# Windowed attention, tile by tile: probabilities are divided by their sums, V becomes the stationary operand, and GpSimd adds the two products of the rotation

## The reference, cut to what matters

```
h = shift_token(x); q, k, v = split(h @ wqkv)        # 8 heads of 64
q, k = l2norm(q) * qs, l2norm(k) * ks
q = q*cos*scale + rotate_half(q)*sin*scale           # k with 1/scale
sim = 8 * q @ k.T, banded; attn = softmax(sim)
x = x + (attn @ v) @ wo
h = layernorm(shift_token(x)) * lg + lb; a, g = split(h @ w1 + b1)
x = x + (a * gelu(g)) @ w2 + b2
```

## Time and profile before

| | |
|---|---|
| median of 3 runs | 429.11 us (429.06 to 431.6) |
| the profiled execution's own time | 431.58 us |
| its span | 429.8 us |
| granted TensorE clock, mean | 0.956 |
| busy over the span: PE, DVE, ACT, POOL | 86%, 81%, 67%, 5% |

### The profile page before, as it was taken

The page is one execution under the profiler, slowest core; times in us unless marked ns, Lnnn a source line. Parts: engine busy times, 40 slices in busy tenths (PEclk is TensorE's granted clock), DMA queues, the critical chain, the costliest instruction groups (busy, mean ns, idle before and its releaser), DMA issues.

```text
span 429.8 us, 10211 instructions
## 1 busy us (share of the span) xinstructions
PE 371.4 (86%) x4104; PEld 272.0 (63%) x4104; DVE 349.4 (81%) x721; ACT 289.1 (67%) x602; POOL 22.8 (5%) x30
## 2 busy tenths in 40 slices
PE   2799999998556789997858999999999999997866
PEld 1488788886511435564435766876767687776845
DVE  5989978986888899886979889888797988884642
ACT  1789998884355457778354666867868777766641
POOL 2000020000020040000000000000000002020110
PEclk9999999999955999999999899999999999998997
DMA  8700010000000000000000000000000000000000
GB/s 325 302 4 4 3 41 3 3 4 3 1 0 1 2 0 2 2 2 0 2 1 2 0 2 0 2 2 0 2 2 1 2 0 2 2 0 2 25 2 24
DMA packets 1774, 8.30 MB, mean 19 GB/s; under 512 B 192, under 2 KB 448, under 8 KB 1472
## 3 DMA queue, kind: packets, MB, share of 16 engines
q1 hardware_dynamic: 1728, 7.65, 4.5%
HBM read 7.12 MB, written 0.52 MB: 18 GB/s over the span
## 4 chain that ended last, share of the span: by engine, by line
PE 48%; DVE 32%; ACT 14%; issue 5%; DMA 1%; DVEq 0%; ACTq 0%
PE ps L252 13%; PE ps L657 5%; ACT blk L1350 3%; PE ps L505 3%; DVE blk L1180 3%; PE ps L630 3%; DVE blk L1171 3%; DVE blk L1162 3%; PE ps L611 2%; PE ps L569 2%; DVE lneg L1187 2%; DVE ss L1172 2%; PE ps L621 2%; PE ps L583 2%; PE ps L492 2%
## 5 line engine op out<-in xcount | busy, mean ns | idle before, releaser
L569 PE MATMUL ps<-w_f,full 128*128 128x512 f32 x96 | 44.7, 599 | 1.4 <-issue 0.9
L1468 ACT ACTIVATE PT<-ps,lneg 128x128 f32<-128x128 f32 x128 | 34.6, 381 | 13.9 <-DVE lneg L1187 13.9
L630 PEld LDWEIGHTS ps<-blk,PT 128*128 128x128 f32 x256 | 30.3, 192 | 0.6
L630 PE MATMUL ps<-blk,PT 128*128 128x65 f32 x256 | 30.4, 272 | 0.0
L252 PEld LDWEIGHTS ps<-blk,st 128*128 128x128 bf16 x768 | 26.8, 98 | 3.8
L1162 DVE TENSOR_TENSOR blk<-ps,tabs 128x1024 f32<-128x1024 f32 x16 | 19.5, 1221 | 11.5 <-ACT blk L1435 11.2
L252 PE MATMUL ps<-blk,rel 128*128 128x64 bf16 x768 | 27.6, 193 | 0.0
L252 PE MATMUL ps<-blk,st 128*128 128x64 bf16 x768 | 27.6, 193 | 0.0
L569 PEld LDWEIGHTS ps<-w_f,full 128*128 128x128 f32 x96 | 16.9, 190 | 16.9 <-issue 16.7
L1022 DVE TENSOR_REDUCE mneg<-ps 128x4 bf16<-128x512 bf16 x32 | 21.9, 686 | 6.6 <-PE ps L357 6.4
L583 PEld LDWEIGHTS ps<-const,blk 128*128 128x128 f32 x128 | 14.8, 146 | 17.3 <-DVE blk L1180 14.6
(11 more groups left out here) (235 smaller groups left out, 913.9 us busy)
## 6 DMA issues: line engine op xcount, KB each, us to landing
w_f<-f_dram SPq DMA_DIRECT2D x2, 1689.0 KB, 13.3
w_x<-l_dram SPq DMA_DIRECT2D x1, 774.0 KB, 6.0
w_f<-ffn_dram SPq DMA_DIRECT2D x1, 561.0 KB, 8.0
X<-x_dram SPq DMA_DIRECT2D x1, 512.0 KB, 3.6
ctxT<-ctxT_dram SPq DMA_DIRECT2D x1, 512.0 KB, 4.5
OT<-maskT_dram SPq DMA_DIRECT2D x1, 512.0 KB, 7.1
rest<-l_dram SPq DMA_DIRECT2D x1, 385.0 KB, 4.2
const<-const_dram SPq DMA_DIRECT2D x1, 324.0 KB, 6.3
```

The costliest lines, as they stand in the source:

```text
L569: m = mm(ps[:, c, :], hT[:, n, :], w_f[:, l, F_QKV + 512 * c:F_QKV + 512 * (c + 1)], start=True, stop=True)
L630: m = mm(ps[:, 5 + h // 4, 65 * (h % 4):65 * (h % 4 + 1)], P1[:, i % 2, P * h:P * (h + 1)], VL[:, i % 3, s, :], start=(h % 4 == 0), stop=T ...
L1468: e = a(S1[:, i % 2, P * k:P * (k + 1)], ps[:, 3 + c, P * j:P * (j + 1)], ACT.Exp, bias=lneg[:, i % 2, k:k + 1])
```

## The change

In `rotate`, the addition of R and T2 leaves VectorE: GpSimd makes it (`sum_pairs`), and `unit_norm` and the next `rotate` wait for it. The exponentials also write their row sums (`accum_out`). VectorE divides the exponentials by them in S1, in two halves of 128x512 (`normalise_p`), before they are transposed. V, without a column of ones, is now the stationary operand (128x64) and the transposed probabilities are streamed; even heads go to output partitions 0 to 63, odd heads to 64 to 127 of bank 5, so that the output comes out transposed. `divide_output`, `turn_o` and the buffer LO are gone. `take_turned_o(i-1)` reads bank 5 and stands ahead of `exponential(i)`; `project_o(i-1)` stands ahead of `turn_p(i)`. The diff, cut to its core:

```diff
@@ TensorE
-            def turn_o(i):
-                pe.wait_ge(sem("lo_norm"), i + 1)
+            def project_o(i):
+                pe.wait_ge(sem("loT"), i + 1)
                 if i >= 1:
                     pe.wait_ge(sem("z"), i)
                 else:
                     pe.wait_ge(sem("res_added"), 6)
                 for j in range(4):
-                    t = tr(ps[:, 7, P * j:P * (j + 1)], LO[:, i % 2, P * j:P * (j + 1)], ident)
-                t.then_inc(sem("loT_ps"), 1)
-
-            def project_o(i):
-                pe.wait_ge(sem("loT"), i + 1)
-                for j in range(4):
                     m = mm(ps[:, 7, 0:P], LOT[:, j, :], ...)
@@ turn_p
-                    pe.wait_ge(sem("lexp"), 2 * i + c + 1)
+                    pe.wait_ge(sem("p_norm"), 2 * i + c + 1)
@@ weigh
+                pe.wait_ge(sem("p_turned"), 2 * i + 2)
                 for h in range(LH):
-                    if h % 4 == 0:
-                        pe.wait_ge(sem("p_turned"), 2 * i + h // 4 + 1)
-                    s = 2 * (h % 4) + h // 4
-                    m = mm(ps[:, 5 + h // 4, 65 * (h % 4):65 * (h % 4 + 1)], P1[:, i % 2, P * h:P * (h + 1)],
-                           VL[:, i % 3, s, :], start=(h % 4 == 0), stop=True, skip_group_check=True)
+                    j, c = h // 2, h % 2
+                    m = mm(ps[64 * c:64 * (c + 1), 5, P * j:P * (j + 1)], VL[:, i % 3, h, :],
+                           P1[:, i % 2, P * (4 * c + j):P * (4 * c + j + 1)],
+                           start=(j == 0), stop=True, skip_group_check=True)
@@ the loop of passes, TensorE
-                    turn_o(i - 1)
+                    project_o(i - 1)
...
-                if i >= 1:
-                    project_o(i - 1)
                 if i >= 4 and i % 2 == 0:
                     hidden(i, (i - 4) // 2)
                 weigh(i)
@@ rotate, VectorE
+                if i >= 1:
+                    dve.wait_ge(sem("pair_sum"), i)
                 step(v.tensor_tensor(heads(R[:, i % 2, :]), u, ...))
...
-                settle()
-                dve.wait_ge(sem("rotated"), i + 1)
-                step(v.tensor_tensor(R[:, i % 2, :], R[:, i % 2, :], T2, ALU.add))
                 step(v.tensor_reduce(ss[:, :], SQ.rearrange("p (h j) -> p h j", j=LD), AX.X, ALU.add))
                 settle()
                 v.tensor_scalar(ss[:, :], ss[:, :], 1e-24, None, ALU.max).then_inc(sem("ss"), 1)
             def unit_norm(i):
                 dve.wait_ge(sem("root"), i + 1)
+                dve.wait_ge(sem("pair_sum"), i + 1)
@@ VectorE, in place of divide_output
+            def normalise_p(i, c):
+                dve.wait_ge(sem("lexp"), 2 * i + c + 1)
+                r = lrec[:, 4 * c:4 * c + 4]
+                step(v.reciprocal(r, lsum[:, i % 2, 4 * c:4 * c + 4]))
+                settle()
+                p = S1[:, i % 2, 512 * c:512 * (c + 1)].rearrange("p (h k) -> p h k", h=4)
+                v.tensor_tensor(p, p, r.rearrange("p (h o) -> p h o", o=1).to_broadcast([P, 4, P]), ALU.mult)\
+                    .then_inc(sem("p_norm"), 1)
@@ the loop of passes, VectorE
-                if i >= 1:
-                    divide_output(i - 1)
                 if 2 <= i + 1 < 2 * NB:
                     unit_norm(i + 1)
+                if i >= 4 and i % 2 == 0:
+                    quarter_rows((i - 4) // 2)
+                normalise_p(i, 0)
                 if i >= 5 and i % 2 == 1:
                     add_down((i - 5) // 2)
-                if i >= 4 and i % 2 == 0:
-                    quarter_rows((i - 4) // 2)
+                normalise_p(i, 1)
@@ ScalarE: take_turned_o, exponential, the loop of passes
-                act.wait_ge(sem("loT_ps"), i + 1)
+                act.wait_ge(sem("lo_ps"), i + 1)
...
-                a(LOT, ps[:, 7, :].rearrange("p (j t) -> p j t", j=4), ACT.Copy).then_inc(sem("loT"), 1)
+                a(LOT, ps[:, 5, :].rearrange("p (j t) -> p j t", j=4), ACT.Copy).then_inc(sem("loT"), 1)
...
-                              bias=lneg[:, i % 2, k:k + 1])
+                              bias=lneg[:, i % 2, k:k + 1], accum_out=lsum[:, i % 2, k:k + 1])
...
+                if i >= 1:
+                    take_turned_o(i - 1)
                 exponential(i)
...
-                if i >= 1:
-                    take_turned_o(i - 1)
@@ GpSimd
+            def sum_pairs(i):
+                pool.wait_ge(sem("rotated"), i + 1)
+                g_.tensor_tensor(R[:, i % 2, :], R[:, i % 2, :], T2, ALU.add).then_inc(sem("pair_sum"), 1)
+
+            for i in range(4):
+                sum_pairs(i)
             for q in range(8):
+                for i in range(4 + 2 * q, min(6 + 2 * q, 2 * NB)):
+                    sum_pairs(i)
...
                 pool.wait_ge(sem("halves"), q + 1)
```

More of the change, by code:

```diff
@@ L153, in build @@
         ymax = sb("ymax", [2])
-        ones = sb("ones", [P])
         wq_i = sb("wq_i", [2, 3, P], BF16)
@@ L179, in build @@
         lr = sb("lr", [2 * LH])
+        lsum = sb("lsum", [2, LH])
         lrec = sb("lrec", [LH])
@@ L216, in build @@
         KT = view(blkf, 7168, 2, 4, P)
-        VL = view(blkf, 9216, 3, LH, LD + 1)
-        LO = view(blkf, 10776, 2, 512)
+        VL = view(blkf, 9216, 3, LH, LD)
         LOT = full[:, 0, 0:512].rearrange("p (a b) -> p a b", a=4)
@@ L577, in turn_qk @@
                 elif i >= 2:
-                    pe.wait_ge(sem("lo_norm"), i - 1)
+                    pe.wait_ge(sem("loT"), i - 1)
                 else:
@@ L676, in last_hidden @@
                 pe.wait_ge(sem("yT"), 14)
-                pe.wait_ge(sem("lo_norm"), 2 * NB)
+                pe.wait_ge(sem("loT"), 2 * NB)
                 for t in range(3):
@@ L787, in _ @@
             turn_norm(16, 6)
-            turn_o(2 * NB - 1)
             hidden_wait(16, 6)
@@ L966, in quantise_weight @@
                 quantise(src, inv, tmp, out, "wq")
-            step(v.memset(ones[:, :], 1.0))
             step(v.memset(less_magic[:, :], -MAGIC))
@@ L1262, in _ @@
             quarter_rows(6)
-            divide_output(2 * NB - 1)
             add_output(2 * NB - 1)
@@ L1534, in _ @@
                 if u == 15:
-                    act.wait_ge(sem("local_zeroed"), 1)
+                    act.wait_ge(sem("scores1"), G * NB)
                     square(0)
@@ L1628, in _ @@
                     i.then_inc(sem("tables") if l == 1 and k == 32 else sem("pool_steps"), 1)
-            pool.wait_ge(sem("scores1"), G * NB)
-            g_.memset(VL[:, :, :, LD:LD + 1], 1.0).then_inc(sem("local_zeroed"), 1)
             bias_row = lambda t: t.rearrange("p (o e) -> p o e", o=1).to_broadcast([P, 2, P])
+            def sum_pairs(i):
[3 more added lines that the diff above has]
+                sum_pairs(i)
             for q in range(8):
+                for i in range(4 + 2 * q, min(6 + 2 * q, 2 * NB)):
+                    sum_pairs(i)
                 l, j = divmod(q, 4)
```

## The result

The changed kernel takes 437.54 us (median of 3 runs, 436.73 to 438.34) against 429.11; the ratio is 1.018, 95% interval 1.015 to 1.020. The forecast was 436.0. The profiled execution is that of 437.54, with a span of 435.8.

What follows compares the result with a forecast made beforehand. A chain of waits round each pair of passes, no full engine, was taken as the bound. Pairs +6.8, start +1.5, layer 1 holds +1.1, end -2.4 made +7.0: 436.0 us, range 418 to 445.

Steps and rivals of the forecast that it cites:

- the hold: VectorE's square-sum clamp after the rotation: blocked 1.2 us by GpSimd's 2.4 us addition, leaving a gain of 0.1.
- the path round the pair: Chain of waits through an even and an odd pass: odd exponentials at 14.6, squares at 17.6, 1.4 late.
- the even pass's zero: End of the largest (L1187 before) in the even pass, from which the forecast times its steps.
- two holds of 0.55 in layer 1: Passes 11 and 13: GpSimd's biases, now behind its sums, reach VectorE's L829; +1.1 in all.
- the pair: One even and one odd steady pass: 25.9 us, 1.3 to 1.4 more; five such pairs +6.8.
- Accumulation: Row sums written by ScalarE's exponentials: 0.12 each, 0.96 for eight.
- the start: Passes 0 to 3: later rotations, less 0.1 each and less add_output's waits for TensorE; +1.5.
- The term of -2.4: Kernel's end: savings from project_o, unit_norm, weighing and last projection, against copy, accumulation and last-half wait; -2.4 with rounding.
- the wait for the last half: At the kernel's end, waiting for the last normalised half of the probabilities: +0.5.
- from the last weighing to the last projection: Stretch at the kernel's end: 3.5 us before, 2.8 left with copy, one third of hidden and L611; -0.7.
- rival without hold: Clamp in the steady pairs not held by GpSimd: pair 23.4, time 418; chance 0.17.

Runs made afterwards that it cites:

- the two kernels near before's usual time: Kernel before with GpSimd's addition of R and T2 alone, 429.84 us; kernel before with VectorE's clamp alone left out, 428.79 us.
- the kernel with the busy end: Changed kernel plus unread TensorE products ahead of turn_qk(15) and behind the loop's last down; 432.83 us, ratio 1.007.

## Why the prediction was right, step by step

**Right: the hold, and what it ends.** The clamp was forecast at 1.4 and to end with GpSimd's sum; it took 1.30 and did. The run without it is the direct test: 18.2 us for an instruction of 0.17. The Trainium skill (SBUF — State Buffer, Who interferes with whom) counts tensor_scalar among those that can block against GpSimd and tensor_reduce among those that never do; both show here, L1162 at 1.30 and L1160 at its usual 1.21 under the same addition.

**Right: the path round the pair.** Against the even pass's zero (290.39) the forecast had rotation at 4.6, clamp done 9.6, odd exponentials 14.6, squares 17.6, rotation 18.7. After: 4.4, 9.3, 14.3, 17.0, 18.1 (294.79, 299.66, 304.68, 307.42, 308.52). The wait ahead of down was 1.5 forecast, 1.6 found. The two holds of 0.55 in layer 1 came too: the last two pairs are 25.75, 0.5 more than the first three.

**Too large: the pair.** 1.36 was forecast and 0.65 measured. Accumulation was sized at 0.12 a piece and is 0.09, 0.24 for eight; 0.3 came from the even pass up to the clamp's end (9.6 for 9.3, of it the rotation's 4.6 for 4.4), and 0.1 from behind the odd squares. The estimate of 0.09 from the Trainium skill (ScalarE: Activation LUTs, What ACT_TABLE_LOAD costs) was the better one. Five pairs with the holds: 7.9 forecast, 4.4 measured.

**About right: the start.** 1.5 was forecast. From the first largest to that of pass 4 it is 0.8 more than in before's profile (218.54 to 263.94, against 218.88 to 263.50), and 1.6 and 1.8 more than in the two kernels near before's usual time.

**Wrong: the end.** The term of -2.4 was mis-sized, and in sign: +1.2 between the profiles, +2.1 to +2.5 against the two kernels near before's usual time. Each piece was priced at full clock. The forecast itself had the waits that lower it (take_turned_o and the read-outs ahead of the last exponentials, the wait for the last half), and the profile before already showed the pattern, at other places of the end. With TensorE kept busy the largest of pass 14 to the end takes 40.3 (391.07 to 431.4), 3.2 less than before's profile (43.5) and about 2 less than the two others. That is near the forecast's -2.4, but it is no proof of its pieces, since the ends of before ran in part at the lower clock as well. One piece didn't come even at full clock: from the last weighing to the last projection 2.8 was forecast, and the kernel with the busy end takes 3.45 (411.48 to 414.93), as long as before's 3.5, because one third of hidden stands ahead of the projection and waits for its own transposes and their copy; the changed kernel takes 5.05 (415.68 to 420.73). So an error of 3.5 (the pairs) and one of about 4.7 (the end) lay on opposite sides, and the total came out 1.5 low. That it came so near is luck; the hold and the path round the pair are not.

**Not seen:** that TensorE's loop was as long as the chain shown. The prediction's rival without hold counted TensorE's gain and the offload together and came out at 418 (measured 419.4), but the expectation for the offload alone on the kernel before, without the clamp, was 5 to 10 us less, where it is 2.7.

What stays open: the only trace of before is of the execution 2.5 us above its median. The two kernels near its usual time differ from it in the rotation, so the split of those 2.5 between the start and the end is close, not exact.

## What to carry to other kernels

Before an elementwise operation goes to GpSimd, read what VectorE runs in its 2.4 us: a 16-column tensor_scalar there waited for its end, and in the changed kernel the addition on GpSimd then saved 0.4 a pair instead of 2.3; without that instruction the ratio went from 1.018 to 0.977. When a part is cut from a chain, look for a second loop of the same length, here TensorE's, before counting the gain (0.9994 for the offload alone, 0.994 without the clamp, and the same pair of 24.57 in both). Price the end of a kernel at the lower clock where TensorE idles ahead of it (2.9 and 4.8 us here), or fill the wait.

## What the runs showed of the hardware beyond expectation

- An exponential that accumulates is followed by an instruction of its own, ACTIVATION_READ_ACCUMULATOR, 0.22 us; it overlaps with its neighbours and adds 0.09 to the pitch of 128x128 exponentials.
- Sixteen products with 64-wide weights on one column half in a row took 0.099 each for 128 streamed columns, and in turn on both halves 0.068; the kernel before had 0.119 (1.90 / 16) with 128-wide weights and 65 columns.
- In one execution with the addition on VectorE, TensorE idled 1.8 us ahead of down in every pair; the granted clock fell behind it in two of the five pairs (0.94 over the pair) and stayed at 1.00 in the other three.
